# A sixth pair convolved by products in a group-norm and 3x3-convolution kernel, with its lines in two buffers and two more evictions on VectorE

## What is computed

```python
def _gn(v, G=32, eps=1e-05):
    g = v.reshape(B_, G, C_ // G, H_, W_)
    m = jnp.mean(g, axis=(2, 3, 4), keepdims=True)
    s = jnp.var(g, axis=(2, 3, 4), keepdims=True)
    return ((g - m) / jnp.sqrt(s + eps)).reshape(v.shape)

x = x + _L0_conv_ref(_gn(x), L0_conv_W)   # weights: sign(W), padding 1
```

## Time and profile before

| | |
|---|---|
| median of three runs (lowest, highest) | 201.97 us (201.77, 202.2) |
| the profiled execution, its own time | 201.95 us |
| its span, first to last instruction | 200.2 us |
| PE busy | 190.6 us, 95% |
| DVE busy | 165.3 us, 83% |
| POOL busy | 166.6 us, 83% |
| ACT busy | 149.8 us, 75% |
| DMA queue of the loads and stores | 73.1% of 16 engines |

### The profile page before, as it was taken

How to read it: one execution, slowest core, us unless ns; L and a number is a source line. 1 busy time by engine, 2 the same in 40 slices (tenths; PEclk the granted TensorE clock), 3 DMA queues, 4 the chain that set the end, 5 groups by cost and what they waited for, 6 DMA issues and landing times.

```text
span 200.2 us, 10044 instructions
## 1 busy us (share of the span) xinstructions
PE 190.6 (95%) x4482; PEld 170.8 (85%) x4482; DVE 165.3 (83%) x363; ACT 149.8 (75%) x142; POOL 166.6 (83%) x85
## 2 busy tenths in 40 slices
PE   1999999999999999999999999999999999999990
PEld 0588889998868988988999988899998999889990
DVE  2899999996999997799988789998769999637392
ACT  3186999799989199899819989963999999595000
POOL 1029886999999999999899997999998899999400
PEclk9999999999999999999999999999999999999999
DMA  6988968950977989779877788887988871906374
GB/s 215 340 302 281 326 207 302 309 177 5 332 254 297 288 348 278 231 257 338 280 251 309 254 330 299 313 264 291 328 289 338 275 283 46 363 11 238 133 279 163
DMA packets 18842, 52.17 MB, mean 261 GB/s; under 512 B 2096, under 2 KB 5296, under 8 KB 18800
## 3 DMA queue, kind: packets, MB, share of 16 engines
q1 hardware_dynamic: 18800, 51.54, 73.1%
HBM read 25.84 MB, written 25.69 MB: 257 GB/s over the span
## 4 chain that ended last, share of the span: by engine, by line
PE 65%; ACT 14%; DVE 13%; DMA 3%; issue 2%; SPq 1%; DVEq 0%; ACTq 0%
PE psum L764 65%; ACT halves L427 5%; ACT xnorm L421 4%; DVE stats L503 4%; DMA xbuf<-in_x_dram 3%; ACT moved L440 3%; DVE xbuf L598 2%; DVE xbuf L584 1%; DVE xbuf L608 1%; ACT line_halves L450 1%; ACT std L416 1%; DVE xbuf L572 1%; ACT lines_norm L454 1%; DVE own L511 1%; DVE halves L566 1%
## 5 line engine op out<-in xcount | busy, mean ns | idle before, releaser
L764 PE MATMUL psum<-halves,w_taps 64*64 64x385 f16 (+8 forms) x4140 | 183.4, 325 | 0.3 <-DVE xbuf L615 0.2
L764 PEld LDWEIGHTS psum<-halves,w_taps 64*64 64x64 f16 x4140 | 158.8, 107 | 16.5 <-ACT moved L440 0.9
L333 POOL TENSOR_TENSOR halves<-xnorm,halves 128x784 f16<-128x784 f32 (+5 forms) x35 | 91.7, 2640 | 19.4 <-ACT xnorm L421 19.1
L503 DVE BATCH_NORM_STATS2 stats<-xbuf 128x6 f32<-128x448 f32 x109 | 59.0, 612 | 3.0 <-DMA xbuf<-in_x_dram 2.8
L427 ACT ACTIVATE halves<-xbuf,coef 128x784 f16<-128x784 f32 (+5 forms) x35 | 50.7, 1448 | 3.1 <-DVE coef L528 2.7
L421 ACT ACTIVATE xnorm<-xbuf,coef 128x784 f32<-128x784 f32 (+5 forms) x35 | 50.4, 1441 | 0.0
L440 ACT ACTIVATE moved<-psum 64x784 f32<-64x784 f32 (+1 forms) x30 | 25.5, 850 | 7.9 <-PE psum L764 7.3
L348 POOL TENSOR_TENSOR xbuf<-xbuf,moved 128x784 f32<-128x784 f32 (+1 forms) x15 | 29.2, 1949 | 0.4 <-ACT moved L440 0.4
L598 DVE SCALAR_TENSOR_TENSOR xbuf<-psum,xbuf 64x784 f32<-64x784 f32 (+1 forms) x32 | 28.2, 881 | 1.0
L584 DVE SCALAR_TENSOR_TENSOR xbuf<-psum,xbuf 128x784 f32<-128x784 f32 x21 | 20.3, 966 | 7.6 <-PE psum L764 7.6
L374 POOL TENSOR_TENSOR line_halves<-lines_norm,line_halves 128x1512 f16<-128x1512 f32 (+1 forms) x10 | 20.9, 2114 | 0.5 <-ACT lines_norm L454 0.5
(11 more groups left out here) (46 smaller groups left out, 74.6 us busy)
## 6 DMA issues: line engine op xcount, KB each, us to landing
xbuf<-in_x_dram SPq DMA_DIRECT2D x47, 448.0 KB, 4.5
out_dram<-xbuf SPq DMA_DIRECT2D x43, 392.0 KB, 3.7
xbuf<-in_x_dram SPq DMA_DIRECT2D x18, 224.0 KB, 4.1
out_dram<-xbuf SPq DMA_DIRECT2D x5, 504.0 KB, 3.5
out_dram<-xbuf SPq DMA_DIRECT2D x5, 448.0 KB, 3.7
out_dram<-xbuf SPq DMA_DIRECT2D x5, 364.0 KB, 4.4
out_dram<-xbuf SPq DMA_DIRECT2D x5, 252.0 KB, 4.2
out_dram<-xbuf SPq DMA_DIRECT2D x1, 224.0 KB, 3.9
```

What stands on the lines that cost most here:

```text
L333: nc.gpsimd.tensor_tensor(at(halves[:, k % HRING, 1, :], a, b), at(xnorm[:, k % NRING, :], a, b), at(halves[:, k % HRING, 0, :], a, b), AL ...
L503: nc.vector.bn_stats(stats[:, n, :], xbuf[:, s, n * STAT:(n + 1) * STAT]).then_inc(blocks_ready, 1)
L764: mm = pe.matmul(outs[:, :, left:right], weights, ins[:, :, left + dx:right + dx], start=first_step, stop=last_step)
```

## The change

Pair 15, the last, becomes a pair with products, with home units rows 43 to 49; products 2 and 1; products 0 and 3; rows 50 to 52; rows 53 to 55, and away units rows 0 to 15; 16 to 21; 22 to 24. `lines` and `line_halves` have two buffers, the f32 scaling writes over `lines` itself, and `lo_lines` is one subtraction of 2016 elements instead of two. For pair 15 VectorE does it, not GpSimd. Away units (13, 1) and (14, 0) are added by VectorE instead of moved by ScalarE and added by GpSimd.

Beside this several orders change. ScalarE's move of (k-1, 0) and GpSimd's add of it stand between the first and the last chunk of pair k instead of after them. GpSimd's add of (1, 1) stands ahead of pair 3's `lo` instead of behind it. `lo_lines` stands ahead of `make_lines` of the next pair. On VectorE, three of the statistics and the aggregation of pair k+2 stand behind the first adds of pair k, in pairs with products behind `add_inner`. Pair 0 loses its own code at the start: four loads instead of five, and the common `scale`; the third coefficient is computed for pairs with products alone.

The core of the diff (pieces that only rename are left out):

```diff
-WINOGRAD = (3, 6, 9, 12, 14)
+WINOGRAD = (3, 6, 9, 12, 14, 15)
+LINES_BY_VECTOR = (15,)
+BY_VECTOR = {(13, 1), (14, 0)}
...
     def home_units(k):
         if k == LAST:
-            return [[(0, 7), (14, 7)], [(28, 7), (42, 4)], [(50, 3)]]
+            return [[(WROW + WROWS, 7)], [2, 1], [0, 3], [(WROW + WROWS + 7, 3)], [(WROW + WROWS + 10, 3)]]
...
     def away_units(k):
         if k == LAST:
-            return [[(7, 7), (21, 7)], [(35, 7), (46, 4)], [(53, 3)]]
+            return [[(0, 8), (8, 8)], [(16, 6)], [(22, 3)]]
...
-        return k != LAST and i == (0 if k in WINOGRAD else 1)
+        return k != LAST and i == (0 if k in WINOGRAD else 1) and (k, i) not in BY_VECTOR
...
-            for n in range(2):
+            for n in range(NPIECE):
                 start_load(sp, 0, n)
-            for (a, b), landing in (((32, 40), first_middle), ((40, 48), loaded[0][2]), ((48, 56), loaded[0][3])):
-                sp.dma_start(at(xbuf[:, 0, :], a, b), at(both(x, 0), a, b)).then_inc(landing, 16)
...
+                if k == LAST:
+                    wait_away(k, 0)
+                    store(k, 0, 0, 16)
+                    sp.wait_ge(home_done, home_before(k) + 3)
+                    store(k, 1, WROW, WROW + WROWS + 7)
+                    sp.wait_ge(home_done, home_before(k) + 4)
+                    wait_away(k, 1)
+                    store(k, 2, 16, 22)
+                    store(k, 3, WROW + WROWS + 7, WROW + WROWS + 10)
+                    sp.wait_ge(home_done, home_before(k) + 5)
+                    store(k, 4, WROW + WROWS + 10, H)
+                    wait_away(k, 2)
+                    sp.dma_start(at(both(out, k), 22, WROW),
+                                 at(xbuf[:, k % XRING, :], 22, WROW)).then_inc(last_stored, 16)
+                    return
...
             def lo_lines(k):
                 n = winograd_before(k)
-                if n:
-                    pool.wait_ge(home_conv, home_blocks_before(WINOGRAD[n - 1], 3))
-                for i, some in enumerate((slice(0, 3 * WN), SUM)):
-                    pool.wait_ge(line_hi_ready, 2 * n + i + 1)
-                    pool.wait_ge(line_norm_ready, 2 * n + i + 1)
-                    nc.gpsimd.tensor_tensor(line_halves[:, 1, some], lines_norm[:, some], line_halves[:, 0, some],
-                                            ALU.subtract).then_inc(line_lo_ready, 1)
+                pool.wait_ge(line_norm_ready, 2 * n + 2)
+                nc.gpsimd.tensor_tensor(line_halves[:, n % 2, 1, :], lines[:, n % 2, :], line_halves[:, n % 2, 0, :],
+                                        ALU.subtract).then_inc(line_lo_pool, 1)
...
-                if k >= 2 and k - 2 not in WINOGRAD and k != WINOGRAD[0]:
+                if k >= 2 and by_scalar(k - 2, 1):
                     add_away(k - 2, 1)
-                for c in range(len(chunks(k))):
+                last = len(chunks(k)) - 1
+                for c in range(last):
                     if (k, c) != (0, 0):
                         lo(k, c)
-                if k >= 2 and k - 2 not in WINOGRAD and k == WINOGRAD[0]:
-                    add_away(k - 2, 1)
+                if k in WINOGRAD:
+                    lo(k, last)
+                if k in WINOGRAD and k not in LINES_BY_VECTOR:
+                    lo_lines(k)
+                if k >= 1 and by_scalar(k - 1, 0):
+                    add_away(k - 1, 0)
+                if k not in WINOGRAD:
+                    lo(k, last)
                 if k == 0:
                     weights_of_products()
                 if k + 1 in WINOGRAD:
                     make_lines(k + 1)
-                if k in WINOGRAD:
-                    lo_lines(k)
-                if k - 1 in WINOGRAD:
-                    add_away(k - 1, 0)
...
             def line_upper(k):
+                act.wait_ge(lines_made, 3 * n + 3)
+                act.wait_ge(offset_ready, n + 1)
...
+                if k in WINOGRAD:
+                    nc.vector.tensor_scalar(coef[:, s, 2:3], own[:, 0:1], -2.0, coef[:, s, 0:1],
+                                            ALU.mult, ALU.mult).then_inc(offset_ready, 1)
...
+            def lo_lines(k):
+                n = winograd_before(k)
+                dve.wait_ge(line_norm_ready, 2 * n + 2)
+                nc.vector.tensor_tensor(line_halves[:, n % 2, 1, :], lines[:, n % 2, :], line_halves[:, n % 2, 0, :],
+                                        ALU.subtract).then_inc(line_lo_ready, 1)
...
+                    if not by_scalar(k - 1, 1):
+                        add_away(k - 1, 1)
+                if k in LINES_BY_VECTOR:
+                    lo_lines(k)
+                begun = 2 if k in WINOGRAD else 4
+                if 1 <= k < NP - 2:
+                    pair_stats(k + 2, range(begun))
                 add_home(k, 0)
-                if k not in WINOGRAD:
+                if k != LAST and not by_scalar(k, 0):
                     add_away(k, 0)
...
+            add_away(LAST, 0)
+            add_outer(LAST)
+            add_home(LAST, 3)
+            add_away(LAST, 1)
+            add_home(LAST, 4)
+            add_away(LAST, 2)
```

More of the change, by code:

```diff
@@ L484, in _ @@
                 if k in WINOGRAD:
+                    hi(k, last)
+                    normalise(k, last)
+                if k >= 1 and by_scalar(k - 1, 0):
+                    move_away(k - 1, 0)
+                if k not in WINOGRAD:
+                    hi(k, last)
+                    normalise(k, last)
+                if k in WINOGRAD:
                     line_upper(k)
```

186 lines of the change are left out of this document (80 added, 106 removed).

## The result

The changed kernel is slower: 206.68 us, median of four executions (206.24 to 207.04), against 201.91 for the kernel before beside it; ratio 1.0228, interval 1.0198 to 1.0257. Its profiled execution took 206.24 us, span 204.4, 4.2 us over the 200.2 before.

The account below looks back on a forecast made before the run. TensorE's columns were taken as the bound from first to last matmul, with GpSimd and VectorE late at the end. 201.95 + 0.4 (pair 13 late) + 3.2 (end later: 1.28 saved against 4.5 of holes) = 205.5 us; range 203.6 to 207.0.

Parts of the forecast that it names:

- both engines late: End of the kernel: GpSimd and VectorE both make TensorE wait; the forecast case, 204.9 to 206.3 us, chance 0.67.
- Start: Pair 0: chain that feeds pairs 1 to 3 comes 0.3 us earlier (0 to 0.6), nothing for TensorE's first step.
- Pair 3: Inside pair 3: new hole of 1.05 us waiting for GpSimd's `lo`, the old 0.80 goes; net +0.25 us.
- Banks of pairs 4, 7, 10, 13: TensorE waits for a bank VectorE's away adds free: 0.05 us at pairs 4, 7, 10, and 0.1 at 13.
- GpSimd: From pair 13's second chunk: input at 162.2, no gap, end at 187.8; `lo` late, hole of 0.45 us in pair 14.
- VectorE: Pairs 14 and 15: product adds hold pair 15's start, outer adds its last block (1.2 us); end 3.2 us later.
- The tail: From the last add to the end, the stores: change put at 0 us (-0.2 to +0.3).
- The sum: Whole kernel: 201.95 + 0.4 + 3.2 = 205.5 us.
- The signs: Changed profile: pair 14 10.5 us, pair 15 13 or more, GpSimd gapless 162.5 to 188, VectorE gapless at end.
- TensorE alone: Rival: TensorE's columns decide, no holes at the end; 201.1 us, some 200.0 without pair 3's hole; chance 0.09.
- GpSimd alone: Rival: in pair 15 VectorE keeps up after 187.85 and only GpSimd is late; 204.2 us, chance 0.14.
- The clock: Rival: TensorE's clock falls in pair 15's holes, costing 1.5 us; 207.0 us; chance 0.08, shared with longer adds.

Follow-up runs that it names:

- the run with both edits: Changed kernel with unit (14, 0) back with ScalarE and GpSimd, and GpSimd's subtraction for pair 14's lines cut to a quarter; 206.49 us.
- the run on pair 3: Changed kernel with GpSimd's addition of (1, 1) put back behind the lower parts of pair 3; 206.72 us.
- the run with short lines: Changed kernel with GpSimd's subtraction for the lines of pair 14 covering only a quarter of its 2016 elements; 206.58 us.

## Why the prediction was right, and where it was not

The forecast, both engines late and 205.5 us, holds in kind; 1.2 us are missing in size. With that the time left the 204.9 to 206.3 that the forecast gave itself and came to lie where 0.08 was put on a falling clock or longer additions. The traces show neither of the two as the reason (1.00 in all holes, additions as long as taken): the mechanism was that of the forecast, with terms that were too small. Step by step:

- **Start.** The forecast took TensorE's first step as unchanged and the profiled execution as the median. In that execution it was 0.18 earlier. But the eleven kernels with this shorter chain (one of them with the loads of before) began between 11.10 and 12.25 (mean 11.68), the three with that of before at 11.02 to 11.43, and 206.24 is the lowest of the four times of the changed kernel: 0.44 of the miss is the median over this execution. The loads' sizes do not explain it. Nor does VectorE's wait for the first pair alone: ahead of its fifth statistic it was 1.30 us where TensorE began at 12.25, and none where it began at 12.07 (the run with both edits). The cause is open.
- **Pair 3.** New hole 1.05 forecast, 1.03 measured; the old one gone (pair 4: 11.82); net +0.25 forecast, +0.22 measured. Right in kind, and the run on pair 3 took the wait away. That the size fits within 0.02 is in part luck: with the same order other traces have 10.96 to 11.57 for pair 3, so a hole of 0.45 to 1.06.
- **Banks of pairs 4, 7, 10, 13.** 0.25 forecast, none measured. Pair 13's was freed at 166.67 and, by the 5.90 us that the step puts into the pair, wanted at 166.67; the estimate was 0.1 late. With the earlier first matmul pair 13 so starts 0.05 late and not 0.4.
- **GpSimd.** Last instruction at 187.8 + 0.4 forecast, 188.45 measured. The input was there at 162.26 (162.2), as the step said, but GpSimd reached it only at 162.64: its lateness has a second cause that the step does not name, the scalings of pair 12's lines. The hole of pair 14 was sized 0.45 (its own dates, 174.5 and 174.1, give 0.4). It is 0.80 by its bracket, and 0.97 by the 11.50 that pair 14 takes in the run with (14, 0) given back, where it is the only hole there, over the 10.53 of before.
- **VectorE.** Away additions 2.21 (2.2 taken), subtraction 2.26 (2.3), the bank at pair 15's start 0.96 late by its bracket (1.1), the last block's 1.06 (1.2). Pair 15 takes 14.15, where the step's own dates give 13.7 (184.7 to 198.4): the outer additions end 12.5 us into the pair and not 12.2, and the last block takes 1.60 (197.83 to 199.43) and not 1.3. The step is also off by 0.2 in itself: 196.9 and 1.3 make 198.2. Last addition +4.15, +3.6 forecast.
- **The tail.** The profiled execution is 4.29 us longer (206.24 and 201.95) and its last addition 4.15 later, so the time behind it grew by 0.14; 0 was taken (-0.2 to +0.3).
- **The sum.** Against the forecast's dates pair 14 starts 0.45 early, pair 14 takes 0.63 more (12.69, where 172.64 to 184.7 is 12.06) and pair 15 0.45 more, and the tail 0.14: with the 0.44 of the start these are the 1.2.
- **The signs.** GpSimd's end (188.45), the move of (12, 0) (157.20, so only just behind 157) and pair 15 came as they should. One sign was wrong as written: 10.5 us for pair 14. By the step's own dates it is 12.06, since the waits for its lower parts and for pair 15's first bank fall into this stretch.
- **TensorE alone** has fallen by the time itself and by the run with five pairs. **GpSimd alone** has fallen by the run with short lines: 3 us less on GpSimd gave 0.61. **The clock** was 1.00 in all holes of the changed kernel's trace, up to 1.48 us long. In two experiments it was not (below).

Of the 3.50 us in the three brackets at and in pair 15, relieving GpSimd gave back 0.6, and taking (14, 0) from VectorE gave back nothing, even where the two engines were kept apart (207.21): the terms of the sum do not come apart one by one.

## What to carry to other kernels

Work taken off the bound engine pays only if each of the others can meet the earlier date: lay their instructions on the clock of the trace, up to the last one, ahead of adding up columns. Where two engines are late for one consumer, an experiment that relieves one of them measures the difference of the two; undo both before you call a part harmless. A wait removed in the middle of a pipeline is worth something only if the engine that caused it is not as late at the next place.

## What the runs showed of the hardware

VectorE's subtraction of two operands in SBUF took 4.10 us beside a GpSimd addition and 2.26 alone. If it did nothing until the addition ended, at 189.39 + 2.08 = 191.47, it would have ended at 193.7; it ended at 193.59. The Trainium skill states this rule ("SBUF — State Buffer", SBUF: two separate sides) for a VectorE operation with two inputs in SBUF and a GpSimd one that reads SBUF: whichever of the two starts first holds the shared ports for its whole instruction and the other is blocked. The trace agrees within 0.14 us. VectorE's product additions, with one operand in PSUM, show no such lengthening beside GpSimd (six in 3.63 us at 182.78, beside GpSimd's lines and lower parts).

TensorE's granted clock fell in the two runs below, to 0.51 and 0.60 over these stretches, that is to 1.2 GHz in most of each, after TensorE had stood still for 1.95 us (until 190.19) and for 2.70 us (until 188.34). First the run with short lines and (14, 0) given back, then the one with GpSimd's addition behind the subtraction:

```profile
191.00:194.50 3.50, 3.50 (x44) 0.51 0.25 93
```

```profile
189.00:193.00 4.00, 4.00 (x56) 0.60 0.00 0
```

In these rows 3.50 us at 0.51 and 4.00 us at 0.60 give 1.7 and 1.6 us less work than the full clock would. Of the second kernel two executions with a mean clock of 0.991 and 0.992 took 207.85 and 207.93 us, two with 1.000 and 0.999 took 206.58 and 206.48. That the fall is what costs these 1.4 us fits, but only the first of the four has a trace, and the mean clock of an execution alone does not tell: the kernel before has executions of 201.37 at 0.995 and 204.33 at 0.999. In the run with (14, 0) given back, holes of 2.71 and 1.77 us left the clock at 1.00, so the length of one hole does not tell either.
